# Attention's first unit begins after two token pairs instead of eight, the other six pairs laid into its first three steps

## The reference

```python
x = x + _L0_xattn_ref(_layernorm(x), ctx_4096, Wq, Wk, Wv, Wo, q_norm_w, k_norm_w)
x = x + _L0_ffn_ref(_layernorm(x), ...)              # 4-bit weights
x = x + _L1_xattn_ref(ctx_4096, _layernorm(x), ctx_4096)
x = x + _L1_ffn_ref(_layernorm(x), ...)              # LoRA experts

# _L0_xattn_ref(latents, context, ...)
kv = jnp.concatenate([context, latents], axis=1)
q, k, v = latents @ Wq, kv @ Wk, kv @ Wv             # 32 query heads, 8 key/value heads of 128
q, k = rms_norm(q, q_norm_w), rms_norm(k, k_norm_w)
probs = softmax(q @ k.T / sqrt(128))                 # 4 query heads share a key/value head
return (probs @ v) @ Wo
```

## Time and profile before

| | |
|---|---|
| median of 3 runs | 1201.81 us |
| the profiled execution | 1201.67 us, of which the span of the trace is 1199.9 us |
| PE busy | 1127.4 us (94%) |
| DVE busy | 755.0 us (63%) |
| ACT busy | 542.7 us (45%) |
| POOL busy | 416.3 us (35%) |
| mean granted clock of PE | 0.978 |

### The profile page before, as it was taken

How to read it: one execution, slowest core, us unless ns; L and a number is a source line. 1 busy time by engine, 2 the same in 40 slices (tenths; PEclk the granted TensorE clock), 3 DMA queues, 4 the chain that set the end, 5 groups by cost and what they waited for, 6 DMA issues and landing times. The chain is left out here.

```text
span 1199.9 us, 19956 instructions
## 1 busy us (share of the span) xinstructions
PE 1127.4 (94%) x6643; PEld 963.4 (80%) x6643; DVE 755.0 (63%) x1572; ACT 542.7 (45%) x1437; POOL 416.3 (35%) x421
## 2 busy tenths in 40 slices
PE   4899999999999999999999988789999999898998
PEld 3799899898899898899899878567777777676776
DVE  7555555555555555555555777799954666687863
ACT  4444554544454544454544544343323445454541
POOL 4433332332322332323332433154422324554531
PEclk7999999999999999999999999999999999798999
DMA  6211111101011101011100010022202245133300
GB/s 210 76 36 33 26 33 32 36 23 35 24 35 32 34 25 35 23 36 32 33 19 11 22 46 1 18 80 80 75 25 54 62 106 124 43 74 77 88 1 36
DMA packets 48731, 56.65 MB, mean 47 GB/s; under 512 B 10822, under 2 KB 29270, under 8 KB 48620
## 3 DMA queue, kind: packets, MB, share of 16 engines
q1 hardware_dynamic: 48620, 55.26, 17.2%
HBM read 40.56 MB, written 2.10 MB: 36 GB/s over the span
## 5 line engine op out<-in xcount | busy, mean ns | idle before, releaser
L387 PE MATMUL bank<-wqkv,kvT 128*128 128x256 f32 x1536 | 201.2, 288 | 8.7 <-DVE vv L577 8.6
L387 PEld LDWEIGHTS bank<-wqkv,kvT 128*128 128x128 f32 x1536 | 189.3, 193 | 10.6 <-DVE vv L577 10.6
L432 PE MATMUL bank<-wo,aoT 128*128 128x512 f32 x768 | 192.0, 399 | 5.7 <-DVE acc L573 5.7
L375 PE MATMUL bank<-wqkv,kvT 128*128 128x512 f32 x768 | 189.2, 396 | 5.6 <-issue 4.0
L375 PEld LDWEIGHTS bank<-wqkv,kvT 128*128 128x128 f32 x768 | 141.7, 191 | 33.2 <-issue 6.2
L432 PEld LDWEIGHTS bank<-wo,aoT 128*128 128x128 f32 x768 | 139.5, 188 | 33.3 <-DVE aoT L568 6.3
L673 POOL TENSOR_TENSOR rms<-msq,half_neg 128x4 f32<-128x4 f32 x64 | 64.4, 1007 | 226.0 <-DVE msq L584 225.8
L560 ACT ACTIVATE prob<-bank,nmax 128x128 f32<-128x128 f32 x256 | 90.3, 372 | 2.1 <-DVE nmax L597 2.1
L538 ACT ACTIVATE qsq<-bank 128x512 f32<-128x512 f32 x64 | 38.2, 597 | 117.0 <-PE bank L375 117.0
L1916 POOL TENSOR_TENSOR pr<-pr,rc 128x512 f32<-128x512 f32 x64 | 66.6, 1044 | 70.7 <-DVE rc L1785 70.6
L676 POOL TENSOR_TENSOR rms<-msq,half_neg 128x2 f32<-128x2 f32 x64 | 44.6, 696 | 134.1 <-DVE msq L593 134.1
(11 more groups left out here) (176 smaller groups left out, 2210.3 us busy)
## 6 DMA issues: line engine op xcount, KB each, us to landing
wqkv_raw<-in_L_xattn_Wq_dram SPq DMA_DIRECT2D x32, 256.0 KB, 2.5
wo_raw<-in_L_xattn_Wo_dram SPq DMA_DIRECT2D x32, 256.0 KB, 2.7
qS<-qhl SPq DMA_DIRECT2D x32, 256.0 KB, 3.8
kS<-chl SPq DMA_DIRECT2D x32, 128.0 KB, 3.0
packed<-_L_ffn_gate_qweight_dram SPq DMA_DIRECT2D x40, 64.0 KB, 2.3
packed<-in_L_ffn_up_qweight_dram SPq DMA_DIRECT2D x40, 64.0 KB, 2.3
packed<-_L_ffn_down_qweight_dram SPq DMA_DIRECT2D x10, 256.0 KB
acc<-in_x_dram SPq DMA_DIRECT2D x8, 256.0 KB, 5.6
```

The source lines that it names most:

```text
L375: mm = pe.matmul(b_q[:, :], kvT[:, l, kt, p, 1:3, :], wqkv[:, par, r, kt, 0:QW], start=(kt == 0 and n == 0), stop=(kt == KT - 1 and n == 2))
L387: mm = pe.matmul(b_kv[:, b * 256:(b + 1) * 256], kvT[:, l, kt, p, 2 * b:2 * b + 2, :], wqkv[:, par, r, kt, QW:QKV], start=(kt == 0 and n = ...
L432: mm = pe.matmul(b_o[:, :], aoT[:, l, h, :, :], wo[:, par, r, h, :], start=(h == 0 and n == 0), stop=(h == G - 1 and n == 2))
```

## The change

`pe_first` now takes pairs 0 and 1 only, and then the steps begin, with unit 0's Q and K as in any other step. Pairs 2 and 3 are laid into step 0, 4 and 5 into step 1, 6 and 7 into step 2, on every engine (`TOKENS`), at fixed places among the step's own work. The banks are chosen anew, from those that the pipeline does not use yet: pairs 5, 6 and 7 share bank 7. The first head's weights are loaded right behind pair 0, into `wqkv_raw` and two more buffers (`qkv_raw0`), each piece with a semaphore of its own; unit 0's Q waits piece by piece. The norm weights are loaded later, and the pieces of Wo are split in steps 1 and 2 instead of at the start (`EARLY`).

```diff
+        qkv_raw0 = at(153056, "qkv_raw0", [P, 2, QKV], F32)
...
+            token_piece(0)
+            for kt in range(KT):
+                qkv_load(first_qkv(kt), 0, kt, s_first_in[kt])
+            token_piece(1)
+            sp.dma_start(wqk[:, 0:1], a["L0_xattn_q_norm_w"].rearrange("(d o) -> d o", o=1)).then_inc(s_nw, 16)
+            sp.dma_start(wqk[:, 1:2], a["L0_xattn_k_norm_w"].rearrange("(d o) -> d o", o=1)).then_inc(s_nw, 16)
+            for p in range(2, 5):
+                token_piece(p)
             wo_piece(0, 0, 0)
             wo_piece(0, 1, 0)
-            qkv_piece(0, 2, 1)
-            qkv_piece(0, 3, 2)
+            for p in range(5, PAIRS):
+                token_piece(p)
             wo_piece(0, 2, 1)
...
-        CTX_BANK = (0, 1, 0, 1, 5, 6, 5, 6)
-        X_BANK = (2, 3, 2, 3, 7, 4, 7, 5)
+        CTX_BANK = (4, 6, 4, 6, 5, 7, 7, 7)
+        X_BANK = (5, 7, 5, 7, 6, 5, 7, 7)
+        TOKENS = {0: (2, 3), 1: (4, 5), 2: (6, 7)}
+        def tokens(st, j, n, part, eng):
+
+            if isinstance(st.i, int) and st.j == j:
+                part(eng, TOKENS[j][n])
+        def pe_context_tokens(pe, p):
+            b = bank[CTX_BANK[p]]
+            pe.wait_ge(sc[p], 16)
...
+            elif p == 6:
+                pe.wait_ge(s_clo, 6)
+            elif p == 7:
+                pe.wait_ge(s_xlo, 7)
...
+        def pe_latent_tokens(pe, p):
+            b = bank[X_BANK[p]]
+            pe.wait_ge(s_xn, p + 1)
...
+            elif p >= 6:
+                pe.wait_ge(s_clo, p + 1)
...
         def pe_first(pe):
             pe.wait_ge(s_const, 4)
+            for p in range(2):
+                pe_context_tokens(pe, p)
+                pe_latent_tokens(pe, p)
             run_steps(pe, pe_step0, HEAD, PERIOD, ROUNDS, STEPS0, pe_ahead)
...
+        EARLY = {0: (), 1: (("wo", 0, 0), ("wo", 1, 0)),
+                 2: (("wo", 2, 0), ("wo", 3, 0), ("qkv", 0, 1)), 3: (("qkv", 1, 1), ("wo", 0, 1))}
...
         def act_first(act):
+            act_context_tokens(act, 0)
+            act_latent_tokens(act, 0)
+            for kt in range(KT):
+                first_hi(kt)
+            act_context_tokens(act, 1)
+            act_latent_tokens(act, 1)
             run_steps(act, act_step0, HEAD, PERIOD, ROUNDS, STEPS0, act_ahead)
...
         def dve_step0(st):
...
+            for j in range(3):
+                tokens(st, j, 0, dve_token_stats, dve)
             if st.has(0, UNITS):
                 dve.wait_ge(s_qsq, st.done(0))
                 wait(dve, s_rq, st.done(1))
                 dve.tensor_reduce(ssq[:, 0:4], qsq[:, :, :], AX, ALU.add).then_inc(s_red, 1)
                 dve.wait_ge(s_red, st.done(0, 2) - 1)
                 dve.tensor_scalar(msq[:, 0:4], ssq[:, 0:4], 1.0 / HD, RMS_EPS, ALU.mult, ALU.add).then_inc(s_qms, 1)
+                for j in range(3):
+                    tokens(st, j, 0, dve_token_apply, dve)
+                tokens(st, 0, 0, dve_context_tokens, dve)
                 dve.wait_ge(s_rq, st.done(0))
...
         def pool_first(pool):
+            ln_power(pool, 0, 0)
+            for n in range(KT):
+                pool.wait_ge(s_wqkv_hi, n + 1)
+                pool.tensor_tensor(wqkv[:, 0, LO, n, :], first_qkv(n), wqkv[:, 0, HI, n, :].bitcast(F32),
+                                   ALU.subtract).then_inc(s_wqkv, 1)
+            ln_power(pool, 0, 1)
             run_steps(pool, pool_step0, HEAD, PERIOD, ROUNDS, STEPS0, pool_after0)
```

More of the change, by code:

```diff
@@ L393, in pe_step0 @@
             pe = nc.tensor
-            if st.has(0, UNITS) and not is_first(st):
+            if st.has(0, UNITS):
                 query_projection(pe, st)
+            tokens(st, 0, 0, pe_context_tokens, pe)
+            tokens(st, 0, 0, pe_latent_tokens, pe)
+            tokens(st, 2, 0, pe_context_tokens, pe)
             if st.has(1, UNITS):
@@ L405, in pe_step0 @@
                 mm.then_inc(s_t, 1)
-            if st.has(0, UNITS) and not is_first(st):
+            tokens(st, 1, 0, pe_context_tokens, pe)
+            tokens(st, 1, 0, pe_latent_tokens, pe)
+            if st.has(0, UNITS):
                 key_projection(pe, st)
+            tokens(st, 0, 1, pe_context_tokens, pe)
+            tokens(st, 0, 1, pe_latent_tokens, pe)
+            tokens(st, 2, 0, pe_latent_tokens, pe)
             if st.has(1, UNITS):
@@ L444, in pe_step0 @@
                 mm.then_inc(s_pv, 1)
+            tokens(st, 2, 1, pe_latent_tokens, pe)
         def weight_piece(st):
@@ new lines, in pieces_of @@
+        def pieces_of(st):
+            if isinstance(st.i, int) and st.j in EARLY:
+                return [(kind, n, ahead, ahead) for kind, n, ahead in EARLY[st.j]]
+            kind, n, g, gj, exists = piece_of(st)
+            return [(kind, n, g, gj)] if exists else []
+        def hi_piece(act, st):
+            for kind, n, g, gj in pieces_of(st):
+                par = gj % 2
+                if kind == "qkv":
+                    act.wait_ge(s_wqkv_in[n % 2], 48 * (2 * g + n // 2 - 1))
+                    wait(act, s_kv, (8 * (g - 1)) if gj >= 2 else 0)
+                    act.activation(wqkv[:, par, HI, n, :], wqkv_raw[:, n % 2, :], ACT.Copy).then_inc(s_wqkv_hi, 1)
+                else:
+                    act.wait_ge(s_wo_in[n % 2], 16 * (2 * g + n // 2 + 1))
+                    wait(act, s_o, (8 * (g - 1)) if gj >= 2 else 0)
+                    act.activation(wo[:, par, HI, n, :], wo_raw[:, n % 2, :], ACT.Copy).then_inc(s_wo_hi, 1)
@@ L593, in dve_step0 @@
                 dve.tensor_scalar(msq[:, 4:6], ssq[:, 4:6], 1.0 / HD, RMS_EPS, ALU.mult, ALU.add).then_inc(s_kms, 1)
+                tokens(st, 2, 0, dve_latent_tokens, dve)
+                for j in range(3):
+                    tokens(st, j, 1, dve_token_apply, dve)
+                tokens(st, 0, 1, dve_context_tokens, dve)
+                tokens(st, 0, 1, dve_latent_tokens, dve)
             if st.has(1, UNITS):
@@ L666, in pool_after0, with pool_token_power @@
             pool_ahead(j)
+        def pool_token_power(pool, p):
+            ln_power(pool, 0, p)
         def pool_step0(st):
             pool = nc.gpsimd
+            for j in range(3):
+                tokens(st, j, 0, pool_token_power, pool)
             if st.has(0, UNITS):
@@ L673, in pool_step0 @@
                 pool.tensor_tensor(rms[:, 0:4], msq[:, 0:4], half_neg[:, 0:4], ALU.pow).then_inc(s_rq, 1)
+                for j in range(3):
+                    tokens(st, j, 1, pool_token_power, pool)
                 pool.wait_ge(s_kms, st.done(0))
```

234 lines of the change are left out of this document (111 added, 123 removed).

## The result

| | before | after |
|---|---|---|
| median, same chip (8 runs before, 7 after) | 1201.51 us | 1206.93 us |
| the profiled execution, and its span | 1201.67, 1199.9 us | 1204.18, 1202.4 us |
| Q of step 4 begins | 69.22 | 69.79 |
| from there to the end of the span | 1130.7 | 1132.6 |

A forecast was written before the change was run, and what follows sets the result against it. PE was taken to bound everything from step 4 on; start 17.5, work 39.3, waits 11.4, clock 1.4 and collisions 0.3 put step 4's Q at 69.9, 0.7 us later: 1202.5 us, range 1197.8 to 1206.6.

The forecast's parts named there:

- The start: Before step 0: unit 0's Q begins at 17.5 instead of 30.12, 12.6 us earlier, with the weight loads hidden.
- rival C: At the start: the weights come late, 1.1 us is lost, 1203.6 us in all; chance 0.08.
- Steps 0 and 1: PE waits for normalized latents behind the unit's own reductions: 1.8 and 1.3 us, then 1.3 and 0.6.
- Step 2: Four token groups share bank 7: PE waits 5.5 us, and the step takes about 15.5 us instead of 10.59.
- 0.3 us for a collision: Steps 1 and 2: DVE's layer norms of pairs 5 and 6 slowed beside POOL's powers, 0.3 us, bounds 0 and 2.0.
- Step 3: K of unit 3 waits 0.9 us for v's high part, behind latents 7 and three weight pieces on ACT.
- The clock: In thin step 2 PE's clock falls once, costing 1.4 us, bounds nothing and 2.3.
- rival B: PE at its lower clock for unit 0's K and all of unit 3's Q: 4.0 us more, 1206.5; chance 0.20.
- Rival A: Lists mesh better: half the 11.4 us of waits and no clock fall, 1195.4 us; chance 0.14.
- Sum of the head: Start, work, waits, clock and collision put step 4's Q at 69.9, 0.7 us later than 69.22.
- Behind the head: From step 4 on everything is bound by PE and keeps its length, so nothing is added there.

The follow-up runs named there:

- after again: The changed kernel run a second time with no edit, against the kernel before: ratio 1.0027.
- the kernel that started Q still earlier: Changed kernel with unit 0's Q ahead of pair 1's latents, and pair 1's power ahead of POOL's last two weight pieces: ratio 1.0018 to before.
- the moved kernel: Changed kernel with 48 fulfilled waits (24 instructions) added in PE's wait for pair 1's context: ratio 1.0006 to the kernel before.
- the filled ones: Changed kernel with 34 unused transposes in step 2 (0.9999), ahead of unit 0's Q (1.0014), or both plus DVE normalizing pairs 2 and 3 earlier (0.9998).
- all six with 602 instructions: Profiles: changed kernel three times (1.0042, 1.0027, 1.0025), with earlier Q (1.0018), with DVE normalizing pairs 2, 3 earlier (1.0023), kernel before plus 22 fulfilled waits (1.0023).
- its third profile: The changed kernel run a third time with no edit, against the kernel before: ratio 1.0025.
- before again: The kernel before run again with no edit, for a second profile: ratio 0.9989 to itself.

## Why the prediction was right and wrong

**The start: right.** Statistics at 3.30 (forecast 3.6), latents 5.67 (5.8), POOL's pieces 8.23 to 15.33 (8.3 to 15.5), Q 17.24 (17.5). ACT took its last weight piece at 10.00, with 0.38 us of wait for its DMA, ahead of the 12.8 at which rival C would have begun: refuted.

**Steps 0 and 1: right.** By pitches, less the 0.4 of the group between, the waits were 1.84 (22.39 to 24.63) against 1.8, then 1.35 against 1.3, 1.24 against 1.3, and 0.46 against 0.6.

**Step 2: right in kind, 1.2 us short.** It took 16.71 us (40.85 to 57.56) where 15.5 were forecast. Waits of 5.5 became 6.9, again by pitches. Half of the difference is K's: 1.4 instead of 0.7. Its row says "issue", so the profile names no releaser; but in PE's list K waits for the low part of v (L632), and that ends at 46.25, 0.1 ahead of K's start at 46.35. DVE was late with it because of this pair, from the timeline of the changed kernel:

```profile
44.09 2.97 POOL L529 TENSOR_TENSOR wo<-wo_raw,wo 128x512 fp32r<-128x512 f32 x2 [3.15 <-ACT wo L518]
...
44.45 1.47 DVE L688 TENSOR_TENSOR prob<-prob,rsum 128x512 f32<-128x512 f32 x1
...
45.84 0.41 DVE L632 TENSOR_TENSOR vv<-bank,vv 128x256 fp32r<-128x256 f32 x1
```

DVE's product of two tiles in SBUF took 1.47 us beside POOL's two low parts of Wo, and 0.69 at 56.80 with POOL idle. The prediction had asked where POOL's pieces of `EARLY` would delay POOL's own powers and not what they would do to DVE. Its 0.3 us for a collision was put on layer norms beside powers, and there was none there: the norm at 24.02 took 0.55 us while POOL's power of the q norm took 1.26 instead of the 1.007 of the earlier trace rows. So the term existed, 0.8 us large, at another instruction. The rule of the Trainium skill, GPSIMD Engine Reference, section Specifications, names DVE instructions with two SBUF inputs, and the product is one: the trace agrees with it, but not at the place where I had used it for 2.0 us.

**Step 3: right.** K of unit 3 waited in the profile of after not at all, since Q came late at the low clock, and in that of after again 0.66 by the row and 0.9 by pitch, as forecast. In the three profiles there is either this wait or the fall of the clock, and the sum had counted both. **The clock: right.** One fall, in step 2, at 1.1 us instead of 1.4, in two of the changed kernel's three profiles. K of unit 0 took 3.12 in all three: rival B did not come, except in the kernel that started Q still earlier. Rival A would have had Q of step 4 before 65: refuted.

**Sum of the head: right, in part by luck.** 69.9 forecast; 69.79, 68.70 and 69.95 measured. By the forecast's own terms Q of step 3 would begin at 56.5 (17.5 + 28.2 of work + 10.5 of waits + 0.3) and did at 57.56; from there to step 4's Q it had 13.4 us (11.08 + 0.9 + 1.4) and 12.2 were measured. The two errors of 1.1 us cancel.

**Behind the head: wrong.** The step that failed is the first: "Everything behind is bound by PE and keeps its length, so the change is worth exactly what it moves the start of step 4's Q". It had a value of 0. In its place the runs show +2.5 us of stalls at two loop turns, +0.6 of clock behind them; another 0.6 of clock at the end of attention may be chance. The range had one sentence for this ("the later layers add some of it, as the places where the clock falls there may shift"), which had no price and the wrong place, behind attention, where nothing was added; of the mechanisms it named the smaller. The slices had been read too favourably, too: the second one of the kernel before, 30 to 60 us, has PE 89% busy at a clock of 0.92, not over 90% at full clock, and from 690 to 750 us PE is 87 to 90% busy and waits for DVE's low part of v.

Could it have been seen? In part. The kernel before has the two rows of issue waits shown above, at the turns of the loop, on the engine that bounds everything; I had read the waits of the first 60 us alone. The one of 0.84 us, ahead of the transposes that follow Q, is the same stall that the change then moves. PE executes two instructions for each matmul row (the page counts 6643 of PE and 6643 of PEld). In the changed kernel the tear is 2 + 7 x 2 = 16 instructions into the loop, two standing ahead of Q; 11 instructions fewer ahead of it put it at 27 in the kernel before, and Q's matmuls end at 2 + 12 x 2 = 26: just in front of the transposes, where the row of L401 stands. With 24 or more instructions added it falls out of the loop's beginning altogether, as in the moved kernel and the filled ones. The page's queue for instructions shows what is fetched there. In a window of 285 to 300 us, of after, and of after moved (queue, kind, packets, MB, share):

```profile
q8 instruction: 3, 0.05, 1.4%
```

```profile
q8 instruction: 2, 0.03, 0.8%
```

One packet less is read around the turn. The same window has 3 packets in both profiles of the kernel before and in all six with 602 instructions, and 2 in the moved kernel after and the three with fillers. Asked in windows of half a microsecond, the three of the changed kernel lie in 290.5 to 291.0, 294.0 to 294.5 and 298.0 to 298.5: Q begins at 293.69 and goes on at 296.75, 2.3 to 3.2 us behind the first and the second. In its third profile the second packet lies a microsecond later, in 295.0 to 295.5, and Q goes on at 297.57. The Trainium skill, Runtime: NRT & Kernel Launch, section Instruction fetch mechanics, states that engines read their instructions in blocks of 256, 16 KiB each, one ahead of the other, and that a taken branch out of the window held breaks this and stalls the engine. The trace agrees: 59 packets of 0.97 MB on that queue are 16.4 KB each, there are 2 us at each turn, and, worked out from the counts above, a second stall where the first block ends too soon behind the branch target. That page, together with the issue rows, would have given a rival here. Its price from the rows of before alone would have been 0 (it comes late enough to be hidden) to about 2 us a turn.

Why a stall behind Q costs less than one inside it follows from the same rows: where Q runs whole, PE has work for 3 us while the next block arrives (in "before again", with its second packet in 293.0 to 293.5 and Q at 4.60 us until 297.3, the second stall is gone). That reading of the sizes rests on the traces and no experiment tested it by itself; that the place decides was tested, in both directions.

## What to carry to other kernels

A change in the part that runs once also moves the code that runs many times: count the instructions ahead of a loop on the bounding engine, and look at the waits for "issue" at its turns before calling the rest unchanged. Where a filler or a harmless edit brings more than its own mechanism can pay for (here 3 us for a clock fall of 1.1), run the same instructions at a place where the mechanism can't act. And earlier work at the start is only worth what the slowest list behind it lets through: here 12.9 us of head start came to nothing within four steps, where DVE serves tokens and units from one list and bank 7 four groups in turn.

## What the runs showed of the hardware that I had not expected

- A loop turn costs PE about 2 us here (1.60 to 2.32 in the rows read at the turns), and a second stall of 0.77 to 2.28 us follows where the loop stands in the program so that Q is torn after 7 matmuls; where it falls 11 instructions deeper into the loop, behind Q, it was 0.84 us or none. Two turns written out gave back 5 us of 1200.
- 22 waits that never wait (11 instructions), at the start of the program, cost 0.2%, from 290 us on.
- DVE's 128x512 product of two SBUF tiles took 1.47 us beside POOL's 128x512 subtraction, and 0.69 without; its 128x512 layer norm, with one such input, 2.04 to 2.10 us beside POOL's 128x768 subtraction, and 0.55 beside a power of 128x4, which itself took 1.26 instead of 1.01.
- Q of unit 0, behind the same thin start, took between 3.94 and 5.39 us in the changed kernel and its variants: where PE's clock rises differs from execution to execution by more than a microsecond of work.
